# Two-layer gated attention and MoE kernel: rotated queries and the folded matrix as two f16 parts each, in three products

## What is computed

```python
x = x + tanh(g_xattn[0]) * L0_xattn(ctx, layernorm(x), ...)   # top-k mixing matrix
x = x + tanh(g_ffn[0])   * L0_ffn(layernorm(x), ...)          # block-sparse GELU MLP
x = x + tanh(g_xattn[1]) * L1_xattn(layernorm(x), ctx, ...)   # 16 heads, latent attention
x = x + tanh(g_ffn[1])   * L1_ffn(layernorm(x), ...)          # 32 experts, top 4, and a shared one
```

```python
q_big  = rope(einsum('bshk,hkq->bshq', q @ Wq.T, w_kc_q))   # 192 columns a head
q_r    = einsum('bshq,hqr->bhsr', q_big, W_qr)
k_r    = einsum('bld,hdr->bhlr', rope(ctx), W_kr)
attn   = softmax(einsum('bhsr,bhlr->bhsl', q_r, k_r))
out    = einsum('bhsd,hkd->bhsk', attn @ rope(ctx), w_kc_kv) ... @ Wo.T
```

## Time and profile before

| | |
|---|---|
| median of 3 runs | 474.87 us |
| profiled execution | 475.87 us, span 474.0 us |
| PE (TensorE matmul) busy | 438.7 us, 93% |
| PEld (weight load) | 279.3 us, 59% |
| DVE (VectorE) | 304.0 us, 64% |
| ACT (ScalarE) | 252.0 us, 53% |
| POOL (GpSimd) | 188.0 us, 40% |
| first layer, up to the stage's end | about 138 us |
| latent attention | 138 to 369 us |

### The profile page before, as it was taken

One profiled execution on the slowest core, in us unless ns is written; L12 is line 12 of the kernel. 1 busy time (PEld: TensorE's weight loads), 2 busy tenths in 40 slices (PEclk: granted clock), 3 DMA queues, 4 the chain that ended last, 5 costly groups with the idle time before them and its releaser, 6 DMA issues. The chain is left out here.

```text
span 474.0 us, 8851 instructions
## 1 busy us (share of the span) xinstructions
PE 438.7 (93%) x2723; PEld 279.3 (59%) x2723; DVE 304.0 (64%) x886; ACT 252.0 (53%) x628; POOL 188.0 (40%) x190
## 2 busy tenths in 40 slices
PE   5886999899969999999999999999998899899987
PEld 2574877786734555555555555555566773644476
DVE  3989799955145766677676667757743748446612
ACT  3582445545314677667767766776666242045510
POOL 1650404041603566555465655546643005543000
PEclk9995999999977999999999999999999979999999
DMA  7643000000102343343334334212200799589202
GB/s 249 190 110 103 3 0 1 1 2 22 46 0 66 90 102 90 77 115 74 94 80 105 89 75 107 50 44 57 66 12 2 204 309 278 143 188 261 72 29 90
DMA packets 61448, 43.81 MB, mean 92 GB/s; under 512 B 22955, under 2 KB 54502, under 8 KB 61414
## 3 DMA queue, kind: packets, MB, share of 16 engines
q1 hardware_dynamic: 60646, 41.04, 32.6%
q0 software_dynamic: 768, 2.36, 2.5%
HBM read 27.25 MB, written 2.23 MB: 62 GB/s over the span
## 5 line engine op out<-in xcount | busy, mean ns | idle before, releaser
L1172 POOL TENSOR_TENSOR PB<-PB,inv 128x512 f32<-128x512 f32 x64 | 66.6, 1041 | 79.6 <-DVE inv L1222 79.4
L1111 ACT ACTIVATE PB<-ps,low 128x256 f32<-128x256 f32 x128 | 59.6, 471 | 31.0 <-DVE low L1216 31.0
L275 POOL TENSOR_TENSOR rot<-rot 128x512 f32<-128x512 f32 x48 | 61.1, 1273 | 32.6 <-DMA rot<-rot 32.6
L1216 DVE TENSOR_REDUCE low<-ps 128x2 f32<-128x512 f32 x64 | 44.1, 689 | 38.4 <-PE ps L1028 37.4
L255 DVE TENSOR_TENSOR rot<-ps,sinq 128x512 f32<-128x512 f32 x48 | 33.2, 692 | 16.6 <-PE ps L242 14.5
L1036 PE MATMUL ps<-ident,PB 128*128 128x128 f32 x256 | 41.1, 283 | 1.1 <-ACT PTS L1119 0.8
L1119 ACT ACTIVATE PTS<-ps 128x512 f32<-128x512 f32 x64 | 38.2, 597 | 7.2 <-PE ps L1036 5.1
L1036 PEld LDWEIGHTS ps<-ident,PB 128*128 128x128 f32 x256 | 27.7, 141 | 24.0 <-issue 19.9
L242 PE MATMUL ps<-XH,CH 128*128 128x512 f16 x96 | 37.6, 392 | 0.0
L242 PE MATMUL ps<-XL,CH 128*128 128x512 f16 x96 | 37.4, 390 | 0.0
L242 PE MATMUL ps<-XH,CL 128*128 128x512 f16 x96 | 37.4, 390 | 0.0
(11 more groups left out here) (246 smaller groups left out, 874.0 us busy)
## 6 DMA issues: line engine op xcount, KB each, us to landing
rot<-rot SPq DMA_DIRECT2D x64, 128.0 KB, 2.3
rot<-rot SPq DMA_DIRECT2D x64, 64.0 KB, 2.0
EGU<-in_L_ffn_W_gate_dram SPq DMA_DIRECT2D x8, 384.0 KB, 5.7
EGU<-in_L_ffn_W_up_dram SPq DMA_DIRECT2D x8, 384.0 KB, 5.8
ED<-in_L_ffn_W_down_dram SPq DMA_DIRECT2D x8, 384.0 KB, 6.6
rot<-in_L_ffn_W_dram SPq DMA_DIRECT2D x2, 1024.0 KB, 10.1
WQ<-in_L_xattn_Wq_dram SPq DMA_DIRECT2D x8, 256.0 KB, 3.0
WO<-in_L_xattn_Wo_dram SPq DMA_DIRECT2D x8, 256.0 KB, 3.1
```

Of the source, the lines that this page charges most:

```text
L275: pool.tensor_tensor(g.RO[:, n, x, :], g.RO[:, n, x, :], g.TC[x][:, :], ALU.add).then_inc(g.sum_ok, 1)
L1111: e = act.activation(PB[t % 2][:, h, :], g.ps[:, SC + t % 2, h * S:(h + 1) * S], ACT.Exp, bias=low[:, t % 2, h:h + 1], scale=-1.0, accum_o ...
L1172: pool.tensor_tensor(PB[t % 2][:, :, :], PB[t % 2][:, :, :], inv[:, t % 2, :].unsqueeze(2).broadcast_to([P, 2, S]), ALU.mult).then_inc(nor ...
L1216: dve.tensor_reduce(low[:, t % 2, :], g.ps[:, SC + t % 2, :].rearrange("p (h s) -> p h s", h=2), AX.X, ALU.min).then_inc(low_ok, 1)
```

## The change

Rotated queries and M are held as two f16 parts each, and the context product is the sum of high x high, high x remainder and remainder x high.

- M becomes MH and ML, scaled by UP = 64: part 4 joins `FOLD_SPLIT`. ACT's copy of M now writes f16, and VectorE subtracts it (`fold_rest`, in step 7 behind the reciprocal), where before VectorE had nothing to do for that part. PE's next part of the fold waits for VectorE instead of ACT.
- The swap and the sum of a group use one f32 tile RS[x] instead of RO[n, x]. Then `rotated_high` (ACT) writes the f16 part RH[n, x] and `rotated_low` (GpSimd) the remainder RL[n, x]. Their steps are in `HIGH` and `LOW`; group 2 is rounded in step 5, group 5 in step 1 of the next pair.
- The swap of a group waits, before it writes RS[x], for the remainder of the group three before it; before, it waited for the context product that had read RO.
- `context_product` waits for the remainders and has twelve f16 matmuls of 512 columns, six over 128 rows and then six over 64 rows, where it had four f32 ones.
- `context_keep` and `context_rest` take out the scale of 64 x 64.
- `norm_stats` counts two of its steps with one semaphore. Waits that count split parts use their number.

```diff
-FOLD_SPLIT = (0, 1, 5)
+FOLD_SPLIT = (0, 1, 4, 5)
...
     if f == 4:
-        return act.activation(g.M[u][:, :, :], o[:, 0:QT * DC], ACT.Copy, scale=1.0 / UP)
+        return act.activation(g.MH[u][:, :, :], o[:, 0:QT * DC], ACT.Copy, scale=UP)
...
-    sp.wait_ge(g.qc_ps, 2 * q + (n - 1 + QCPS0))
+    sp.wait_ge(g.ro_low, GROUPS_Q * q + (k - QT + 1 + LOW0))
     for at in range(0, P, 2 * w):
-        sp.dma_start(g.RO[at:at + w, n, x, :], g.TS[x][at + w:at + 2 * w, :]).then_inc(g.swap_ok[x], 16)
-        sp.dma_start(g.RO[at + w:at + 2 * w, n, x, :], g.TS[x][at:at + w, :]).then_inc(g.swap_ok[x], 16)
+        sp.dma_start(g.RS[at:at + w, x, :], g.TS[x][at + w:at + 2 * w, :]).then_inc(g.swap_ok[x], 16)
+        sp.dma_start(g.RS[at + w:at + 2 * w, x, :], g.TS[x][at:at + w, :]).then_inc(g.swap_ok[x], 16)
...
-    pool.tensor_tensor(g.RO[:, n, x, :], g.RO[:, n, x, :], g.TC[x][:, :], ALU.add).then_inc(g.sum_ok, 1)
+    pool.tensor_tensor(g.RS[:, x, :], g.RS[:, x, :], g.TC[x][:, :], ALU.add).then_inc(g.sum_ok, 1)
+
+
+def rotated_high(act, g, q, k):
+
+    n, x = k // QT, k % QT
+    act.wait_ge(g.sum_ok, GROUPS_Q * q + (k + 1 + SUM0))
+    act.wait_ge(g.qc_ps, 2 * q + (n - 1 + QCPS0))
+    act.activation(g.RH[:, n, x, :], g.RS[:, x, :], ACT.Copy).then_inc(g.ro_high, 1)
+
+
+def rotated_low(pool, g, q, k):
+
+    n, x = k // QT, k % QT
+    pool.wait_ge(g.ro_high, GROUPS_Q * q + (k + 1))
+    pool.tensor_tensor(g.RL[n][:, x, :], g.RS[:, x, :], g.RH[:, n, x, :], ALU.subtract).then_inc(g.ro_low, 1)
...
-    pe.wait_ge(g.sum_ok, GROUPS_Q * q + (QT * n + QT + SUM0))
+    pe.wait_ge(g.ro_low, GROUPS_Q * q + (QT * n + QT + LOW0))
     pe.wait_ge(g.qc_ok, 2 * q + (n + QC0))
-    for h in range(2):
-        pe.matmul(g.ps[HI[h], QP, :], g.M[u][:, h, :], g.RO[:, n, h, :], start=True, stop=False)
-    for h in range(2):
-        mm = pe.matmul(g.ps[HI[h], QP, :], g.M[u][HI[h], 2, :], g.RO[HI[h], n, 2, :], start=False, stop=True)
+    terms = split(g.MH[u], g.ML[u], g.RH[:, n], g.RL[n])
+    for m, (mx, rx) in enumerate(terms):
+        for h in range(2):
+            pe.matmul(g.ps[HI[h], QP, :], mx[:, h, :], rx[:, h, :], start=(m == 0), stop=False)
+    for m, (mx, rx) in enumerate(terms):
+        for h in range(2):
+            mm = pe.matmul(g.ps[HI[h], QP, :], mx[HI[h], 2, :], rx[HI[h], 2, :], start=False, stop=(m == 2))
...
-        m = dve.tensor_tensor(g.Q[h][u][HI[1 - h], cols], g.ps[HI[h], QP, :], g.Q[h][u][HI[h], cols], ALU.subtract)
+        m = dve.scalar_tensor_tensor(out=g.Q[h][u][HI[1 - h], cols], in0=g.ps[HI[h], QP, :], scalar=1.0 / (UP * UP),
+                                     in1=g.Q[h][u][HI[h], cols], op0=ALU.mult, op1=ALU.subtract)
...
+        HIGH = {3: (0, 1), 7: (3, 4)}
+        LOW = {3: (0, 1), 4: (2,), 7: (3, 4)}
...
-                for k in range(QT, GROUPS_Q):
-                    summed(0, k)
-                pairs(pool, step, cross)
+                summed(0, QT)
+                for k in range(QT, GROUPS_Q - 1):
+                    summed(0, k + 1)
+                    rotated_low(pool, g, 0, k)
+                pairs(pool, step, cross, head)
...
                     inverse(p, t)
+                    if folds and t == LAST:
+                        fold(p + 2, u, FOLDS - 2)
```

More of the change, by code:

```diff
@@ L497, in _ @@
                             add_partners(pool, g, 0, n - 1)
+                for k in range(QT):
+                    rotated_low(pool, g, 0, k)
             @block.tensor
@@ L784, in _ @@
                             second_norm(b - 1)
+                for k in range(QT):
+                    rotated_high(act, g, 0, k)
                 norm_root(act, g, n2, B - 1)
@@ L1139, in step, with head @@
                         turned(p, t - 1)
+                def head(p, u, t, asks, folds):
+                    for k in range(QT, GROUPS_Q):
+                        if t == min(1, k - QT):
+                            rotated_high(act, g, 0, k)
+                    step(p, u, t, asks, folds)
                 def cross(p, u, t, asks, folds):
@@ L1154, in _ @@
                     fold(1, 1, f)
-                pairs(act, step, cross)
+                pairs(act, step, cross, head)
                 turned(PAIRS - 1, LAST)
@@ L1179, in step, with head @@
                         summed(p + 1, SUMMED[t])
+                    if asks:
+                        for k in LOW.get(t, ()):
+                            rotated_low(pool, g, p + 1, k)
+                def head(p, u, t, asks, folds):
+                    step(p, u, t, asks, folds)
+                    if t == 0:
+                        rotated_low(pool, g, 0, GROUPS_Q - 1)
                 def cross(p, u, t, asks, folds):
```

55 lines of the change are left out of this document (37 added, 18 removed).

## The result

The changed kernel takes 488.2 us, the kernel before beside it 474.6: the ratio is 1.0236, with a 95% interval of 1.020 to 1.0271.

What follows compares the result with a forecast made beforehand. TensorE was taken to bound the attention; 4.4 + 0.2 + 1.15 - 0.44 + 2.1 + 0.8 = 8.2 us slower gave 484.1 us on the profiled execution, which lies 1.0 above the median, so 483.1 us; range 477 to 490.

Steps and rivals of the forecast that it cites:

- falls of the clock in the pairs: Rival: the new waits make TensorE's clock fall in every pair, adding 10 us, to 493 us; chance 0.10.
- What bounds the kernel: In the attention's pairs TensorE is the bound, busy for all 27.80 us; GpSimd rises to 23.4 and does not become it.
- The product: Context product on TensorE: twelve f16 products, in pairs side by side, take 1.54 us instead of 2.02, 0.48 less.
- The rival in which its matmuls don't run side by side: Context product takes 2.83 us instead of 1.54 at 512 columns, kernel 504 us; chance 0.04.
- The links: ACT's rounding, GpSimd's remainder and handovers, in series from a sum's end to its context product: 1.99 us.
- hidden links: Rival: rounding and remainder are hidden before the context products and the kernel is faster, 467.2 us; chance 0.08.
- links at their lower ends: Rival: rounding and remainder 0.36 us cheaper at 14 places, no change that can be measured, 477.2 us; chance 0.12.
- The pairs: Pairs 1 to 6: group 5's product adds 0.73 us a pair (+4.4), group 2's 0.03 (+0.2).
- The start: End of the first layer: GpSimd subtracts three groups one after the other before the product, which starts after 134.14: +2.1 us.
- The last pair: Last pair, with shorter steps: first context product +1.15 us, second -0.44.
- The head: Head of the attention: M's remainder, roundings and remainders delay the product by 1.28 us less 0.48, +0.8.
- the forecast's last link: Head of the attention: the product waits for remainder 5, ending at 157.5, and starts at 157.55 against 156.27.

Runs made afterwards that it cites:

- kernel with the other last pair: Kernel with both edits, but in the last pair GpSimd normalises before sum 5 and takes group 4's remainder behind it: 475.4 us, ratio 0.9994.
- kernel with both edits: Changed kernel with sums 2 and 5 ahead of the normalisations, group 5 rounded earlier, first layer's three remainders on VectorE: 475.35 us, ratio 0.9989.

## Why the prediction was right, and where it was off

The forecast was 483.1 us, 8.2 slower, in a range of 477 to 490; measured are 488.2. That it lies inside the range is in part luck: the upper part was meant for GpSimd at 1.27 us, which measured 1.16, and for falls of the clock in the pairs, which didn't come, while what filled it were the last pair and the part behind the attention.

- **What bounds the kernel.** Right. TensorE bounds the pairs and waits only where a product waits for the chain; seven more operations on each of GpSimd and ACT elsewhere moved the last product by 0.1 us.
- **The product**, 1.54 us forecast: 1.53. TensorE's busy time fell by 7.6 us against the 7.7 worked out. The rival in which its matmuls don't run side by side, at 2.83 us, is ruled out.
- **The links**, 1.99 us forecast: 1.95 (0.03 + 0.63 + 0.08 + 1.16 + 0.05). The remainder, scaled from two narrower ones, is exact; ACT's rounding is 0.03 dearer than the copy it was priced by the earlier trace rows and its handover cheaper by as much and more. So hidden links, and links at their lower ends, are out.
- **The pairs**, 0.76 a pair forecast: 0.86. Step 2's products came 1.17 late by starts (1.21 forecast), step 6's 0.65 (0.51). The 0.14 that step 6's is over its forecast lie in one handover: GpSimd, in order of time, ends this remainder at 200.63 + 1.15 = 201.78, and the product starts at 202.02, 0.24 later, where step 2 shows 0.05. Why that is so wasn't found.

```profile
200.63 1.15 POOL L298 TENSOR_TENSOR XN<-rot 128x512 f16<-128x512 f32 x1 [0.74 <-ACT rot L291]
```

  The waits are as they were forecast, about 1.2 and 0.5: 1.10 and 0.58 us of idle time, put down to GpSimd.
- **The start**: +2.1 forecast, +1.67 measured, the product at 133.70 against 134.14. By the sum's start (128.99, before 129.34) the timeline runs 0.35 us early, the three remainders take 3.39 us where 3.48 were put, and the rest of the step is right.
- **The last pair**, +0.71 forecast, +2.06 measured. This is the step that failed. The forecast costed the remainders of groups 0, 1, 3 and 4 at nothing, since "GpSimd would be idle and nothing is asked of them". In full pairs that holds, but barely: the normalisation behind two remainders still waits for VectorE's reciprocal, 0.39 and 0.18 us.

```profile
183.68 1.04 POOL L1219 TENSOR_TENSOR PB<-PB,inv 128x512 f32<-128x512 f32 x1 [0.39 <-DVE inv L1281]
...
197.62 1.04 POOL L1219 TENSOR_TENSOR PB<-PB,inv 128x512 f32<-128x512 f32 x1 [0.18 <-DVE inv L1281]
```

  In the last pair steps are shorter, and two remainders in series hold up the normalisation behind them, and so the sum. GpSimd of the kernel after, in order of time:

```profile
351.39 1.04 POOL L1219 TENSOR_TENSOR PB<-PB,inv 128x512 f32<-128x512 f32 x1 [1.90 <-DVE inv L1281]
352.39 2.28 POOL L298 TENSOR_TENSOR XN<-rot 128x512 f16<-128x512 f32 x2
354.62 1.04 POOL L1219 TENSOR_TENSOR PB<-PB,inv 128x512 f32<-128x512 f32 x1
355.62 1.27 POOL L283 TENSOR_TENSOR rot<-rot 128x512 f32<-128x512 f32 x1
357.63 1.15 POOL L298 TENSOR_TENSOR XN<-rot 128x512 f16<-128x512 f32 x1 [0.74 <-ACT rot L291]
```

  From 351.39 on GpSimd runs without a pause until it waits for ACT's rounding, so nothing ahead of sum 5 was free. Before, the same sum waited 0.41 us for its DMA; now it starts 10.48 us after the previous product where it started 10.02 after, with that product 0.48 shorter: 0.94 late, exactly what the second product is over its forecast. At the first product of the pair the same reckoning gives 0.42 (the sum starts 10.54 us after the previous product before and 10.48 now, plus 0.48), and the product is 0.41 over its forecast. The kernel with the other last pair confirms the reading. It has there the order of the changed kernel but for one remainder, moved behind the sum:

```profile
343.23 1.04 POOL L1222 TENSOR_TENSOR PB<-PB,inv 128x512 f32<-128x512 f32 x1
344.37 1.27 POOL L283 TENSOR_TENSOR rot<-rot 128x512 f32<-128x512 f32 x1
345.59 2.27 POOL L298 TENSOR_TENSOR XN<-rot 128x512 f16<-128x512 f32 x2
```

  Its sum starts 9.51 us after the previous product (334.86) instead of 10.48, about the 10.02 of before less the 0.49 of the cheaper product. The second product follows the first after 13.11 us instead of 13.75: 0.64 earlier and not 0.97, as the moved remainder now stands in the chain. (The 1.05 us above are against the kernel with both edits, whose last pair has another order again.)
- **The head**, 1.31 with the first wait of step 6: 1.45, and that is luck in part. M's remainder held up the fold's last product by 0.39 more (0.82 instead of 0.43, forecast 0.37), and remainder 4 stood ahead of the normalisation of tile 0, for which TensorE waited 2.52 us where before it waited 0.19. But the product did not then wait for remainder 5, as the forecast's last link had it: this ended at 157.86, the product started at 158.70, since the transposes and scores ahead of it took 1.90 us at low clock (0.57 over 156 to 160) where before they took 1.02. By its start the product is 0.76 late against the attention's start, not 1.28, and the rest came behind it, where it took 2.05 us at low clock. Before, the clock was low at other times (137 to 144 and 150 to 154, now 139 to 143 and 156 to 160), so that the chain's part can't be read apart. A small slip in the forecast: 151.55 + 0.37 + 0.60 are 152.5, not 152.4.
- **The rest of the program**, nothing forecast, +2.7. No term of the sum looked behind the attention. The clock was a rival there only as a fall in every pair, and in the changed kernel's pairs it stayed at 1.00 with gaps of up to 1.98 us (in the one execution with the remainders on VectorE it did fall in the last pair, over 346 to 350). It fell once more elsewhere, behind the longer wait for the indirect load. Why that load lands later is not settled: over all these kernels, the one before included, the time from the start of the last pair's second product to the end of the span is 124.9 to 131.1 us, though the code of that part is the same, and the two longest (131.1 both) have two more stretches of low clock in it than the kernel before, which has one.

So the mechanism and its prices held in the full pairs and at the start, and of the 4.2 us between forecast and measured (12.4 against 8.2) 1.35 are the last pair's order, 2.7 the part behind the attention, and the small terms cancel but for 0.15.

## What to carry to other kernels

Splitting an operand to make a matmul cheaper puts the rounding and the remainder in series ahead of it: count the latency from the last input's arrival to the matmul, not the engines' free time, and reorder the engine that makes them (here one normalisation into the gap where the other engine rounds) together with the split. Work that is costed at nothing because an engine is idle there must be looked at where steps are shortest, in the first and the last turn of the loop; how much room there is can be read from what the next instruction behind it waits for (here 0.18 to 0.39 us in full pairs, nothing in the last). And if the gain is then some microseconds in the loop, check what the same operations cost in the prologue, where nothing covers them: in the kernel with both edits start, head and last pair took back 4.1 of the 4.4 us that six pairs gave.

## What the runs showed of the hardware

- **VectorE and GpSimd hold each other up** when both read operands from SBUF: a 128x512 subtraction on VectorE took 0.69 us alone and 1.72 to 1.75 beside GpSimd, whose sum took 1.73 instead of 1.27. The Trainium skill (SBUF — State Buffer, on the two separate sides) says that a VectorE operation with two SBUF inputs and a GpSimd operation that reads SBUF take one shared pair of ports in turn, whole instructions at a time. The trace agrees: the 1.03 us that VectorE's grew by is somewhat less than one of GpSimd's (1.27), the 0.46 of GpSimd's sum somewhat less than one of VectorE's (0.69), as when an instruction starts while the other engine's is under way.
- **A change between products of 128 and of 64 rows costs 0.12 us**, measured by four more of them in 0.48 us. The Trainium skill (TensorEngine Tiling (Array Packing), Key Properties) says that changing the mode drains the engine; the 0.12 us agree with a cost at each change, though the trace doesn't show the draining itself.
- **One GpSimd subtraction costs 0.20 us over 8 columns, 0.67 over 256 and 1.16 over 512**: about 0.19 us at any width and 1.9 ns a column, an estimate from these three.
- **Handing over is cheap, being handed over in series isn't**: GpSimd to ACT 0.03 us, ACT to GpSimd 0.08, GpSimd to TensorE 0.05 (about 0.1 in the last pair, 0.24 in step 6), together 0.16 of a chain of 1.95.
